# Keys turned by DMA, an earlier routing tail, the expert number ahead, and routed rows normalised on GpSimd, in a two-layer attention kernel with experts

## What is computed

```python
x, l = layer_norm(image_embeds, ln1_g, ln1_b), layer_norm(latents, ln2_g, ln2_b)
q = l @ Wq                                   # latents are x of the kernel, images the context
k, v = jnp.split(jnp.concatenate([x, l], axis=1) @ Wkv, 2, axis=-1)
...                                          # softmax attention of 16 heads over 64 + 64 rows, @ Wo, added to x
```

## Time and profile before

| | us |
|---|---|
| three runs | 1626.33, 1629.28, 1632.08 |
| median | 1629.28 |
| the profiled execution | 1624.12 |
| its span, first to last instruction | 1622.3 |
| busy: PE, DVE, ACT, POOL | 1390.7, 1318.4, 1283.3, 1074.1 |

### The profile page before, as it was taken

How to read it: one execution, slowest core, us unless ns; L and a number is a source line. 1 busy time by engine, 2 the same in 40 slices (tenths; PEclk the granted TensorE clock), 3 DMA queues, 4 the chain that set the end, 5 groups by cost and what they waited for, 6 DMA issues and landing times. The chain is left out here.

```text
span 1622.3 us, 52403 instructions
## 1 busy us (share of the span) xinstructions
PE 1390.7 (86%) x16800; PEld 1179.2 (73%) x16800; DVE 1318.4 (81%) x3902; ACT 1283.3 (79%) x3936; POOL 1074.1 (66%) x1524
## 2 busy tenths in 40 slices
PE   4798899965999999999999999999998188888860
PEld 3677777744888888888888888888886077676750
DVE  3689999885998999999999999999996256565657
ACT  2388888874999999999999999999996166565535
POOL 2478877654666788778877887788875545554550
PEclk9899999997999999999999999999999589999975
DMA  4455544200000000000000000000000134332309
GB/s 151 143 183 210 183 156 185 93 3 25 14 13 12 16 22 25 19 18 20 23 18 18 20 23 20 18 18 23 16 11 18 33 73 77 71 74 61 69 27 311
DMA packets 138950, 101.79 MB, mean 63 GB/s; under 512 B 72184, under 2 KB 119835, under 8 KB 138800
## 3 DMA queue, kind: packets, MB, share of 16 engines
q1 hardware_dynamic: 119200, 78.52, 16.0%
q0 software_dynamic: 8640, 16.93, 3.5%
q10 hardware_dynamic: 10960, 4.46, 1.0%
HBM read 30.09 MB, written 57.16 MB: 54 GB/s over the span
## 5 line engine op out<-in xcount | busy, mean ns | idle before, releaser
L1316 ACT ACTIVATE c_p<-bank,c_nmax 128x128 f32<-128x128 f32 x1024 | 368.9, 401 | 1.9 <-DVE c_nmax L1170 1.2
L1105 POOL TENSOR_TENSOR c_p<-c_p,c_rden 128x512 f32<-128x512 f32 x256 | 266.8, 1042 | 110.1 <-DVE c_rden L1180 105.7
L1316 ACT ACTIVATION_READ_ACCUMULATOR c_p<-bank,c_nmax 128x1 f32 x1024 | 244.1, 241 | 0.0
L1501 POOL DMA_INDIRECT moe_outputs<-e_y,e_to x142 | 146.3, 1031 | 140.3 <-DVE e_y L1527 105.9
L1563 ACT ACTIVATE e_h<-bank,moe_b 128x256 f32<-128x256 f32 x284 | 117.9, 468 | 103.5 <-remote 65.2
L112 PE MATMUL bank<-c_kvT,qk_fused 128*128 128x128 f16 x1024 | 186.0, 220 | 10.8 <-ACT c_kvT L1295 10.4
L1170 DVE TENSOR_REDUCE c_nmax<-bank 128x4 f32<-128x512 f32 x256 | 173.6, 678 | 17.4 <-PE bank L114 14.2
L113 PE MATMUL bank<-c_kvT,qk_fused 128*128 128x128 f16 x1024 | 185.8, 220 | 0.0
L114 PE MATMUL bank<-c_kvT,qk_fused 128*128 128x128 f16 x1024 | 185.8, 220 | 0.0
L1386 PE MATMUL bank<-const,c_p 128*128 128x128 f32 x1024 | 156.0, 275 | 3.2 <-DVE c_pT0rest L1191 1.7
L1148 POOL DMA_INDIRECT moe_slots<-r_rows,r_pos x128 | 131.8, 1030 | 34.8 <-issue 34.8
(11 more groups left out here) (331 smaller groups left out, 5880.5 us busy)
## 6 DMA issues: line engine op xcount, KB each, us to landing
moe_slots<-slot_fill SPq DMA_DIRECT2D x66, 520.0 KB, 5.6
f_z<-moe_outputs SPq DMA_DIRECT2D x32, 256.0 KB, 5.0
x<-in_x SPq DMA_DIRECT2D x16, 256.0 KB, 3.1
a_ctx<-in_ctx SPq DMA_DIRECT2D x32, 128.0 KB, 3.0
moe_stage<-in_L_ffn_W SPq DMA_DIRECT2D x16, 256.0 KB, 3.1
c_rows<-in_ctx SPq DMA_DIRECT2D x128, 32.0 KB, 2.0
c_rows<-x SPq DMA_DIRECT2D x128, 32.0 KB, 1.8
out_x<-x ACTq DMA_DIRECT2D x16, 256.0 KB, 6.3
```

The lines of the kernel that those rows point to most:

```text
L1105: pool.tensor_tensor(pr[r % 4][:], pr[r % 4][:], rep(rden[r % 4][:], 2, P), ALU.mult).then_inc(m["pn"], 1)
L1316: last = act.activation(pr[r % 4][:, h, :], SB[r % 2][:, P * h:P * h + P], ACT.Exp, bias=nmax[r % 4][:, h:h + 1], accum_out=den[r % 4][:, ...
L1501: pool.indirect_dma_start(s.z, bass.IndirectOffsetOnAxis(ap=to[t % YBUF][:, h:h + 1], axis=0), ys[t % YBUF][:, h, :], None, bounds_check=2 ...
```

## The change

The keys and values of a tile are turned by a DMA transpose that SP issues, from `c_kv_parts` straight to `c_kvT`, with four buffers in place of two; the transposes on TensorE and the copy on ScalarE are gone. SP loads two tiles' rows with each set of four DMAs. The routing stages stand four steps earlier, and for the last three groups earlier still (the second and third number in each tuple), with `r_rows`, positions and a semaphore of their own (`own(g)`). GpSimd normalises the rows of a group with two operations (an addition, a multiplication) in place of ScalarE's four. On VectorE `c_kv` stands behind the reduction of its step. In the experts TensorE reads the number of the next tile in the middle of `first`. The first layer and `combine` are unchanged.

```diff
-    c_loaded = [sem(f"c_ctx_loaded{n}") for n in range(4)]
+    c_loaded = [sem(f"c_ctx_loaded{n}") for n in range(2)]
+    kvt_in = [sem(f"c_kvt_in{n}") for n in range(4)]
...
-    scattered = sem("r_scattered")
+    scattered = [sem(f"r_scattered{n}") for n in range(4)]
...
-        cs = [sb(f"c_rows{n}", [P, 2, D]) for n in range(4)]
+        cs = [sb(f"c_rows{n}", [P, 2, 2, D]) for n in range(2)]
...
-        kvt = [sb(f"c_kvT{n}", [P, 2, 4, 64], F16) for n in range(2)]
+        kvt = [sb(f"c_kvT{n}", [P, 2, 4, 64], F16) for n in range(4)]
...
-        rows = sb("r_rows", [P, GT, ROW], F16)
+        rows = [sb(f"r_rows{n}", [P, GT, ROW], F16) for n in range(4)]
...
-        AT_STATS, AT_RSTD, AT_KVN, AT_KV, AT_KVT, AT_G, AT_S, AT_PN, AT_PT, AT_O, AT_W, AT_X3 = 15, 13, 12, 11, 7, 6, 3, 2, 0, -1, -5, -9
-        ROUTE_STATS = 14
-        ROUTE_RSTD, ROUTE_XN, ROUTE_XT, ROUTE_LOGITS, ROUTE_TOP, ROUTE_INDEX, ROUTE_MASK = 27, 32, 34, 38, 39, 42, 43
-        ROUTE_HIGH, ROUTE_LOW, ROUTE_STEP, ROUTE_BASE, ROUTE_POS = 44, 47, 45, 46, 47
+        AT_STATS, AT_RSTD, AT_KVN, AT_KV, AT_G, AT_S, AT_PN, AT_PT, AT_O, AT_W, AT_X3 = 15, 13, 12, 11, 6, 3, 2, 0, -1, -5, -9
+        EVEN = GROUPS - 3
+        ROUTE_STATS = 10
+        ROUTE_RSTD, ROUTE_XN, ROUTE_XT, ROUTE_LOGITS = (23, 23, 23), (28, 28, 24), (30, 29, 25), (34, 30, 26)
+        ROUTE_TOP, ROUTE_INDEX, ROUTE_MASK = (35, 31, 27), (38, 32, 28), (39, 32, 28)
+        ROUTE_HIGH, ROUTE_LOW, ROUTE_STEP = (40, 29, 25), (43, 30, 26), (41, 33, 29)
+        ROUTE_BASE, ROUTE_POS = (42, 33, 29), (43, 34, 30)
         AT_KV_LOW = AT_KV - 1
-        ROUTE_SCATTER = (48, 50, 51, 52, 54, 55, 56, 58)
-        FIRST, LO, HI, LAST = -15, 64, 240, CHUNKS + 43
+        ROUTE_SCATTER = tuple(zip((44, 46, 47, 48, 50, 51, 52, 54), (39, 40, 42, 43, 44, 46, 47, 48), (33, 34, 35, 36, 38, 39, 40, 41)))
+        FIRST, LO, HI, LAST = -15, 64, 224, CHUNKS + 26
...
+        def own(g):
+
+            return max(g - EVEN + 1, 0) if known(g) else 0
...
         @block.sync
         def _(sp):
...
+            def load(n):
+                if n >= 2:
+                    sp.wait_ge(m["kvn"], 2 * n - 2)
                 for half in range(2):
                     rows = slice(64 * half, 64 * half + 64)
-                    sp.dma_start(cs[k][rows, 1 - half, :], cvw[1 - half, t, :, :]).then_inc(c_loaded[k], 16)
-                    sp.dma_start(cs[k][rows, half, :], s.xg(i)[rows, k, :]).then_inc(c_loaded[k], 16)
-            walk(sp, 0, TILES, 4, 4, TILES, step)
+                    to = cs[n % 2]
+                    sp.dma_start(to[rows, :, 1 - half, :], cvw[1 - half, 2 * n:2 * n + 2, :, :].rearrange("t s d -> s t d")).then_inc(c_loaded[n % 2], 16)
+                    sp.dma_start(to[rows, :, half, :], s.xg(n // 2)[rows, 2 * (n % 2):2 * (n % 2) + 2, :]).then_inc(c_loaded[n % 2], 16)
+
+            def turn_keys(v):
+                sp.wait_ge(m["kv"], v + 1)
+                if v >= 4:
+                    sp.wait_ge(m["s"], 4 * (v - 3))
+                sp.dma_start_transpose(kvt[v % 4][:].rearrange("p n a c -> p (n a c)").rearrange("p (b c) -> p b c", b=4),
+                                       kvs[v % 4][:].rearrange("p n b d -> p (n b d)")).then_inc(kvt_in[v % 4], 16)
+
+            load(0)
+            load(1)
+            for v in range(TILES):
+                turn_keys(v)
+                if v % 2 == 1 and v + 3 < TILES:
+                    load((v + 3) // 2)

         @block.gpsimd
...
                     pool.tensor_tensor(r_rstd[:], r_rstd[:], s.mhalf[:, 0:GT], ALU.pow)
+                if (g := group(i, k, ROUTE_XN)) is not None:
                     pool.drain()
-                    pool.tensor_tensor(r_nb[:], r_nb[:], r_rstd[:], ALU.mult).then_inc(mr["rstd"], 1)
+                    wait(pool, mr["xt"], g)
+                    pool.tensor_tensor(r_xn[:], s.xg(g), rep(r_nb[:], 2, D), ALU.add)
+                    pool.drain()
+                    pool.tensor_tensor(r_xn[:], r_xn[:], rep(r_rstd[:], 2, D), ALU.mult).then_inc(mr["xn"], 1)
...
         @block.vector
...
+                if t := tile(i, k, AT_KVN):
+                    v, r, g = t
+                    a, b = mv[r % 2], rst[r % 2]
+                    dve.wait_ge(m["rstd"], v + 1)
+                    wait(dve, m["kv"], v - 3)
+                    for n in range(2):
+                        last = dve.tensor_scalar(kv[r][:, n, :], cs[r // 2][:, r % 2, n, :], a[:, n, 0:1], b[:, n:n + 1], ALU.subtract, ALU.mult)
+                    last.then_inc(m["kvn"], 1)
                 if (g := group(i, k, ROUTE_TOP)) is not None:
...
         @block.scalar
...
-                if t := tile(i, k, AT_KVT):
-                    v, r, _ = t
-                    act.wait_ge(m["kvt"], v + 1)
-                    wait(act, m["s"], 4 * (v - 1))
-                    act.activation(kvt[r % 2][:].rearrange("p n a c -> p (n a c)"), KVB[:, 0:512], ACT.Copy).then_inc(m["kvt_copied"], 1)
...
                 if (g := group(i, k, ROUTE_HIGH)) is not None:
-                    wait(act, scattered, 128 * g)
-                    act.activation(rows[:, :, 0:D], r_xn[:], ACT.Copy).then_inc(mr["row_high"], 1)
-                if (g := group(i, k, ROUTE_XN)) is not None:
-                    act.wait_ge(mr["rstd"], g + 1)
-                    wait(act, mr["row_done"], g)
-                    for j in range(GT):
-                        last = act.activation(r_xn[:, j, :], s.xg(g)[:, j, :], ACT.Identity, bias=r_nb[:, j:j + 1], scale=r_rstd[:, j:j + 1])
-                    last.then_inc(mr["xn"], 1)
+                    if own(g) == 0:
+                        wait(act, scattered[0], 128 * g)
+                    act.activation(rows[own(g)][:, :, 0:D], r_xn[:], ACT.Copy).then_inc(mr["row_high"], 1)
...
         @block.tensor
...
-                if t := tile(i, k, AT_KVT):
...
-                    for part in range(2):
-                        for b in range(2):
-                            at = 2 * P * part + P * b
-                            last = pe.transpose(KVB[:, at:at + P], kvs[r][:, part, b, :], s.ident_h[:])
-                    last.then_inc(m["kvt"], 1)
...
-                    if r % 4 == 0:
-                        pe.wait_ge(m["kvt_copied"], 4 * i + (k + AT_G) // 4 + 1)
+                    if u := tile(i, k, AT_G):
+                        pe.wait_ge(kvt_in[u[1]], 16 * (u[2] + 1))
...
+            def of_tile(t):
+                return pe.value_load(tab[0:1, 0, t:t + 1], min_val=0, max_val=EXPERTS - 1)
+
             def first(t, e):
...
                 for b in range(KB):
+                    if b == 2:
+                        ahead = of_tile(t + 1) if t + 1 < NTILE else None
...
-            of = [None, None]
+            of = [None, None, of_tile(0)]
             for t in range(NTILE + 2):
-                now = pe.value_load(tab[0:1, 0, t:t + 1], min_val=0, max_val=EXPERTS - 1) if t < NTILE else None
-                if t < NTILE:
-                    first(t, now)
+                ahead = first(t, of[2]) if t < NTILE else None
```

More of the change, by code:

```diff
@@ L1044, in cross_attention @@
         tx = sb("r_tx", [P, 72])
-        dest, first_choice = (rows[:, :, 2 * D + at:2 * D + at + 2].bitcast(F32) for at in (0, 2))
+        dest, first_choice = ([part[:, :, 2 * D + at:2 * D + at + 2].bitcast(F32) for part in rows] for at in (0, 2))
         block = ctx.enter_context(nc.Block())
@@ L1205, in step @@
                     dve.bn_aggr(mv[r % 2][:, 1, :], bst[:, 1, :]).then_inc(m["stats"], 1)
-                if t := tile(i, k, AT_KVN):
-                    v, r, g = t
-                    a, b = mv[r % 2], rst[r % 2]
-                    dve.wait_ge(m["rstd"], v + 1)
-                    wait(dve, m["kv"], v - 3)
-                    for n in range(2):
-                        last = dve.tensor_scalar(kv[r][:, n, :], cs[r][:, n, :], a[:, n, 0:1], b[:, n:n + 1], ALU.subtract, ALU.mult)
-                    last.then_inc(m["kvn"], 1)
                 if t := tile(i, k, -ROUTE_STATS):
                     v, r, g = t
+                    if not tile(i, k - 1, AT_STATS):
+                        dve.drain()
                     dve.bn_stats(r_bn[:, r, :], s.xg(g)[:, r, :])
```

80 lines of the change are left out of this document (35 added, 45 removed).

## The result

The changed kernel takes 1665.94 us (median of 4 runs, 1664.82 to 1668.31), the kernel before beside it 1630.05. The ratio is 1.0232, 95% interval 1.0202 to 1.0262: **slower by 2.3%, some 36 us**. I had forecast no change, 1628 us, range 1586 to 1652, so the result lies outside the range and on the side of rival B, above its 1648. The profiled execution took 1668.31 us with a span of 1666.4; against the span before, 1622.3, it is 44.1 us longer.

What follows compares the result with a forecast made beforehand. TensorE and VectorE were taken as close to the pace together, 53.6 us per group, GpSimd slightly behind. +2 + 14 - 1 - 12 - 4 = -1 us against the profiled 1624.12; with the median 5.2 higher, 1628 us, range 1586 to 1652.

Steps and rivals of the forecast that it cites:

- rival B: Attention groups: slower by lock and jitter, c_kv pairs as long as today, 56.2 us per group, 1648 us; 17 in 100.
- signs that I had named: Trace signs of being right: r_pick 54.2 to 55.3 us apart, named engine waits, transpose landings, experts 30 to 34 us behind attention.
- the sum of the ring: Attention: VectorE and GpSimd waiting for each other take 54.7 us per group in place of 53.6, +14 us over 13 groups.
- VectorE's half: Ring leg on VectorE from c_kv to c_rden seven steps later: 23.63 us, before savings of up to 0.4 a pair.
- GpSimd's half: Ring leg on GpSimd from c_p to c_rstd eight steps later: 28.73 us without idle, plus 2.3 new, 31.0.
- Rival A: Attention: the ring does not bind and TensorE's savings count, -26 us in 16 groups, 1589 us; 28 in 100.
- TensorE's savings: Attention: 0.9 us of transposes and 0.7 of copy waits per group, lost in the ring, counted in the rival without it.
- point of decision: Attention: the slower rival decides from 54.8 us per group, where 13 groups eat up the tail and the experts.
- The head: First tile: the DMA transpose stands in place of transposes and copy, +2 us, bounds +1 and +5.
- First 28 steps: Attention steps ahead of the first group's normalising: TensorE's saving counts there, -1 us.
- The tail: From the last attention product to the experts: own rows for the last groups shorten it, -12 us, bounds -6 and -14.
- The expert number: Experts: reading it ahead removes TensorE's seam before each tile, -4 us, bounds 0 and -10.

Runs made afterwards that it cites:

- experiment 1: Changed kernel with VectorE's c_kv pair back at the end of its step; ratio 1.0014 to the kernel before, group 53.8 us.
- Experiment 2: Changed kernel with normalising back on ScalarE and c_kv left in mid-step; ratio 0.9963 to the kernel before, group 53.4 us.
- experiment 6: Changed kernel with GpSimd's two normalising operations three steps earlier and r_rows at steps 39 and 40; ratio 1.0038 to the kernel before, group 53.8 us.
- experiment 10: Changed kernel with c_kv still in mid-step but behind the reciprocal c_rden; ratio 1.0141 to the kernel before, group 55.2 us.
- experiment 7: Kernel before with only the keys turned by DMA transpose, loads one tile at a time; ratio 1.0011 to the kernel before, group 54.1 us.
- experiment 8: Changed kernel with c_rstd computed one step earlier on GpSimd; ratio 1.0122 to the kernel before, group 55.4 us.
- experiment 13: Changed kernel with ten unread TensorE products per group filling its wait ahead of c_p's transposes; ratio 1.0183 to the kernel before, group 56.1 us.
- experiment 11: Kernel before with only the change's tail (routing offsets, rows and semaphores); ratio 0.9945, 1559.93 us beside 1566.7, group 53.7 us.
- experiment 3: Changed kernel with both c_kv back at the end of its step and normalising back on ScalarE; ratio 0.9989 to the kernel before, group 54.2 us.
- experiment 4: Kernel before with only TensorE's expert number read in the middle of first; ratio 0.9994 to the kernel before.

## Why the prediction was wrong

**The mechanism was right.** Four of the signs that I had named are in the trace: c_kv idle for c_rstd, most behind the new pair (3.29 us; I had said some 3), TensorE idle for c_pT rest, the transposes landing in 2.4 to 3.2 us, one wait for c_kvT. Two are not: r_pick comes 57.1 us apart, and the experts' first product 37.2 us behind the last product of attention instead of 30 to 34. Experiments 1, 2 and 6 show that neither part costs anything like this without the other or in another step.

**The step that failed is the sum of the ring**, the term of 54.7 us per group with bounds 54.2 and 55.3. By the rows above, the same sum is now: GpSimd from 940.79 to 974.94, 34.15 us; 0.13 to c_kv; VectorE from 975.07 to 998.23, 23.16; 0.25 to the next c_p at 998.48. That is 57.69, the distance of the two c_p. VectorE's half was right (23.63 less the savings). GpSimd's half was put at 31.0 and is 3.1 larger. Of these, 1.9 us are waits for c_rden that only the groups with the lower clock have (1.54 and 0.37), 0.5 is the wait at 944.81 that all have, and 0.6 are longer gaps inside c_rstd (0.64 and 0.54 where 0.26 and 0.30 stood). Over the seven groups GpSimd's half is 33.4 us on average.

I had taken today's waits, 0.85 and 0.29, out of the leg as if a ring that binds left no idle time in it. It does. The 0.50 us stand behind VectorE's pair of c_kv, which runs from 943.49 to 944.64 ahead of the reciprocal; with the pair behind it, in experiment 10, this wait is gone. The longer gaps come with the keys by DMA, from 6.2 to 13.2 us in 400 in experiment 7. In experiment 8, with the same transposes and c_rstd one step earlier, none of the 29 gaps between its first two operations is over 0.14 us, so the step counts here too. Why, I can't say.

How much of the miss is which? The mean group is 56.9, 2.2 over my 54.7. Experiment 2 has the same ring without the two operations, at 53.4, where my sum less 2.3 gives 52.4: **1.0 us was missing before the new work came in**, in the waits and gaps just named. With the two operations and the clock at 1.00 (experiment 13) it is 56.1, 2.7 more for what I had at 2.3: another 0.4. The clock is the last 0.8.

**What I did not have at all is the clock.** TensorE's stops were under 1 us before and the clock 1.00, so nothing in the trace of before gave a price. The case of 13 puts it at 0.8 us per group, and the seven groups of the one trace (five with the lower clock, 57.3 us on average, two without, 55.9) at 1.4 for a group that has it, 1.0 on average. The 8.1 us behind the last whole group come from the same meeting of the two parts. Counted alike, that stretch is 78.0 us in the changed kernel, 71.4 and 71.9 in experiments 2 and 11, with normalising on ScalarE, and 73.6 in experiment 1, with c_kv at the end of its step. In experiment 6, which moved the operations of the steady groups and not those of the last three, it is still 77.2.

**Rival A** (the ring does not bind, 1589 us) had a second mistake: without the ring, TensorE's 1.6 us per group would have counted. Experiments 1, 3 and 7 show groups of 53.8, 54.2 and 54.1. In 3 and 7 VectorE sets the pace, by pairs of c_kv that take 0.6 to 2.3 us according to what GpSimd runs beside them; what set it in the kernel before, where TensorE was busy for 394.7 of 400 us, no run shows. I had read "TensorE and VectorE are close to the pace together" and then given TensorE's savings a value in 28 of 100 cases. **Rival B** had the right sign, and its point of decision, 54.8 us per group, was passed by 2.3. Its reasons did not come true: the c_kv pairs became shorter (0.72 us on average, 0.98 before), and the group is no 1.2 us longer than its ring, since the ring's sum above is the group to the last digit.

The Trainium skill's rule of "SBUF — State Buffer", section "SBUF: two separate sides", says that VectorE in a two-port mode and GpSimd lock each other out of their shared ports for a whole instruction. By that rule a pair beside c_p lasts until c_p is over; the rows of experiment 8 agree (1.86 us, c_p inside it), and so do the 0.60 us of experiment 6, where no such operation runs. I had used it to lengthen the pair and not to ask in which steps the pair meets c_p. The Trainium skill's page "VectorE: DVE Perf Modes", section "The three transpose paths", gives 1309 ns for a block by DMA, from which I had estimated 5.2 us for four. The trace disagrees with my estimate: the whole transpose lands 2.5 us after its issue (2.4 to 3.2, for the 32 whose landing is in the trace), so blocks don't add up, and the first tile is delayed by 1.3 us only (2.7 from GpSimd's last operation to the first product, 1.4 before).

**The head** (+2, measured +3.8): 1.3 are the transpose, the rest is an earlier or later end of the first layer, which lay 4 us apart in the two profiles of the changed kernel. **First 28 steps**, -1: measured -1.4. **The tail**, -12 with bounds -6 and -14: measured -8.3 with normalising on GpSimd and -10 to -12 in experiment 11. In the last group GpSimd's two operations stand alone on the path, with a scatter ahead of them. The stretch itself came out inside its bounds. **The expert number**, -4 with bounds 0 and -10: measured 0, by experiment 4. The seam went and the stops moved into the tile, as the profile's "issue" and ScalarE waits there had warned.

## What to carry to other kernels

A wait that is put in the middle of an in-order engine's step is priced by everything behind it in that step, and by who waits for that; if the releasing engine waits in turn for something queued behind, look for the third engine through which the stall can come home (here only where TensorE's clock fell), and leave the idle times of the ring in the sum. When two parts of a change meet in one ring, each of them alone proves nothing: 2.3 us of work cost 3 us per group in one step and, with r_rows moved along, almost nothing three steps earlier. And a saving on an engine that shows 99% busy is worth nothing until the trace shows who waits for it.
